# Queries and keys of an attention kernel: copied from tile to tile per term in place of a trip through DRAM, with their projections moved close to their use

## What is computed

```python
qkv = x @ w_qkv                                  # x: 4, 512, 256
q, k, v = (qkv[:, :, 0], qkv[:, :, 1], qkv[:, :, 2])
scores = jnp.einsum('bqhd,bkhd->bhqk', q / scale, k)
scores = jnp.where(causal_mask[None, None], scores, NEG)
attn = jax.nn.softmax(scores, axis=-1)
out = jnp.einsum('bhqk,bkhd->bqhd', attn, v) @ w_out
```

## Time and profile before

| | us |
|---|---|
| time, median of 3 runs | 477.55 |
| lowest and highest | 477.39, 483.26 |
| span of the profiled execution, first to last instruction | 420.8 |
| PE busy in it | 377.7 (90%) |
| DVE busy | 287.1 (68%) |
| POOL busy | 235.4 (56%) |
| DMA, mean rate over the span | 178 GB/s |

### The profile page before, as it was taken

One profiled execution on the slowest core, in us unless ns is written; L12 is line 12 of the kernel. 1 busy time (PEld: TensorE's weight loads), 2 busy tenths in 40 slices (PEclk: granted clock), 3 DMA queues, 4 the chain that ended last, 5 costly groups with the idle time before them and its releaser, 6 DMA issues.

```text
span 420.8 us, 10405 instructions
## 1 busy us (share of the span) xinstructions
PE 377.7 (90%) x2894; PEld 223.1 (53%) x2894; DVE 287.1 (68%) x1009; ACT 242.4 (58%) x534; POOL 235.4 (56%) x374
## 2 busy tenths in 40 slices
PE   5979999999999999997989899988999999989780
PEld 2526554444565445653444466665676777665230
DVE  1157767887879789889799489763666666643562
ACT  2431566667555776556857447562666666556842
POOL 5422144444223888227872855777777766646762
PEclk9999999999999999999999999996999999999987
DMA  4858555646751282649547435636655554429693
GB/s 137 261 192 231 172 165 173 189 136 209 213 164 29 90 277 91 190 144 276 176 149 224 138 123 149 189 132 195 188 175 169 165 158 145 129 69 369 235 375 118
DMA packets 54071, 74.78 MB, mean 178 GB/s; under 512 B 9842, under 2 KB 45308, under 8 KB 52480
## 3 DMA queue, kind: packets, MB, share of 16 engines
q1 hardware_dynamic: 46832, 56.93, 45.7%
q0 software_dynamic: 6912, 16.93, 11.0%
q10 hardware_dynamic: 272, 0.26, 0.2%
HBM read 46.33 MB, written 29.66 MB: 181 GB/s over the span
## 4 chain that ended last, share of the span: by engine, by line
PE 64%; DVE 16%; issue 7%; DMA 6%; ACT 3%; SPq 1%; POOL 1%; ACTq 0%; DVEq 0%
PE PS L697 12%; PE PS L868 8%; PE PS L719 7%; PE PS L821 6%; PE PS L790 5%; PE PS L847 5%; PE PS L665 5%; PE PS L804 3%; DVE MX L1425 2%; PE PS L928 2%; PE PS L710 2%; PE PS L898 2%; DMA YL<-scratch_y 2%; DMA scratch_qk<-PA 1%; DMA scratch_y<-Y,XG 1%
## 5 line engine op out<-in xcount | busy, mean ns | idle before, releaser
L1139 ACT ACTIVATE PT<-PS 128x512 f32<-128x512 f32 x160 | 92.0, 596 | 41.7 <-PE PS L847 36.9
L1783 POOL DMA_INDIRECT scratch_y<-Y,XG x80 | 79.5, 994 | 35.6 <-issue 18.2
L1755 POOL TENSOR_SCALAR_AFFINE_SELECT PT<-PT 128x256 f32<-128x256 f32 (+1 forms) x140 | 50.1, 367 | 78.0 <-ACT PT L1139 76.3
L1774 POOL DMA_INDIRECT scratch_slots<-XP,RI x64 | 63.8, 997 | 35.1 <-DVE XP L1368 16.1
L821 PE MATMUL PS<-KS,QS 96*128 96x512 bf16 (+3 forms) x256 | 61.7, 302 | 10.9 <-DVE MX L1432 4.6
L697 PE MATMUL PS<-W,XGT 128*64 x320 | 61.8, 337 | 1.2 <-DVE WG L1289 0.7
L847 PE MATMUL PS<-QS,KS 98*128 98x512 bf16 (+3 forms) x256 | 60.9, 299 | 1.5 <-ACT PT L1139 1.5
L699 PE MATMUL PS<-WG,XGT 128*64 128x192 f32 x320 | 61.9, 338 | 0.0
L1353 DVE SCALAR_TENSOR_TENSOR HH<-PS,XG,SG 128x96 f32<-128x96 f32 x80 | 24.9, 316 | 35.7 <-ACT SG L1061 31.0
L697 PEld LDWEIGHTS PS<-W,XGT 128*64 128x64 f32 x320 | 41.2, 139 | 13.7 <-issue 9.0
L821 PEld LDWEIGHTS PS<-KS,QS 96*128 96x128 bf16 x256 | 21.4, 99 | 44.7 <-DVE MX L1432 16.7
(11 more groups left out here) (237 smaller groups left out, 718.3 us busy)
## 6 DMA issues: line engine op xcount, KB each, us to landing
XG<-scratch_slots SPq DMA_DIRECT2D x160, 65.0 KB
scratch_qk<-PA SPq DMA_DIRECT2D x14, 384.0 KB, 3.4
W<-in_gate_up_dram SPq DMA_DIRECT2D x16, 288.0 KB
KS<-scratch_qk SPq DMA_DIRECT2D x32, 128.0 KB, 3.5
YL<-scratch_y SPq DMA_DIRECT2D x8, 512.0 KB, 7.0
QS<-scratch_qk SPq DMA_DIRECT2D x8, 384.0 KB, 3.7
QS<-scratch_qk SPq DMA_DIRECT2D x24, 128.0 KB, 3.6
W<-in_down_dram SPq DMA_DIRECT2D x8, 288.0 KB
```

The costliest lines, as they stand in the source:

```text
L1139: e.activation(PT[:, p % NPT, n, :], PS[:, 2 + (rank[u] - 1) % 2, :], ACT.Exp).then_inc(st_exp, 1)
L1755: e.affine_select(out=d, in_=d, compare_op=ALU.is_ge, fill=0.0, base=0, pattern=[[0, 1 if n < 2 else 2], [1, 128]], channel_multiplier=-1) ...
L1774: e.indirect_dma_start(out=XS[:, :], out_offset=bass.IndirectOffsetOnAxis(ap=RI[:, b % 2, TOPK * q + n:TOPK * q + n + 1], axis=0), in_=XP[ ...
L1783: e.indirect_dma_start(out=YK[:, :], out_offset=bass.IndirectOffsetOnAxis(ap=XG[:, j % NXG, D + 1:D + 2].bitcast(I32), axis=0), in_=Y[:, j ...
```

## The change

The scratch tensor in DRAM is gone. A unit `lay` takes the place of `qkout` and `load`: for each of its projection's terms, as soon as that term is there, it copies PA straight into each row of QS or KS where the term is wanted, one DMA of 128 KB per row, six per unit. The lists QS_TERMS and KS_TERMS say which rows take which term. A `lay` first waits until the group three before has done its last `st`, since it writes that group's place of QS and KS. ACT may write a place of PA when the six copies of the unit two before have landed.

The projections of group g stand at the slots 20g - 18 (queries) and 20g - 12 (keys), for all groups from 2 on. Nothing of sequence 1 is projected ahead of slot 0. The values of sequence 1 stand whole at the slots 5 and 9, `xg` of sequence 0 whole at 13. The ones and the input of sequence 1 are issued on SP only behind the four `lay` of sequence 0. The halves of units are gone.

```diff
-QS_ROWS = ((0, 2, 3, 0), (1, 6, 1, 1), (3, 6, 1, 1), (5, 6, 1, 2))
-KS_ROWS = ((0, 3, 2, 1), (1, 6, 1, 0), (2, 6, 1, 0), (5, 6, 1, 0), (4, 6, 1, 2))
+TERMS = 6
+QS_TERMS = ((0, 2, 4), (1, 3), (5,))
+KS_TERMS = ((1, 2, 5), (0, 3), (4,))
+COPIES = 16 * TERMS
...
-    plan = [("inputs",), ("xt", 1)]
+    plan = [("inputs",)]
...
-            put(slot + 3, ("qkout",) + u[1:])
+            put(slot + 3, ("lay",) + u[1:])
...
-                plan += [(kind, 0, m) for kind in ("qk", "resid", "part", "qkout")]
-            plan += [("load", 0), ("v", 0, 0), ("v", 0, 1)]
+                plan += [(kind, 0, m) for kind in ("qk", "resid", "part", "lay")]
+            plan += [("v", 0, 0), ("v", 0, 1)]
...
+            plan += [("ones",), ("xt", 1)]
...
+            for c in range(2):
+                put(5 + 4 * c if b == 1 else VALUES_AT[b - 2] + 2 * c, ("v", b, c))
             if b == 1:
...
+                put(13, ("xg", 0))
+            for half in range(2):
+                put(20 * (2 * b + half) - 18, ("qk", b, half))
+                put(20 * (2 * b + half) - 12, ("qk", b, 2 + half))
...
-    for g in range(2, 2 * B):
-        put(5 * (4 * g - 3), ("load", g))
...
+        def laid(b, m):
+
+            return (ks_in if m >= 2 else qs_in)[m % 2], COPIES * (b + 1)
...
+                elif kind == "lay":
                     b, m = a
-                    r = (rank[u] - 1) % 2
...
+                    g = 2 * b + m % 2
+                    r, rows = (rank[u] - 1) % 2, (KS if m >= 2 else QS)[g % RG]
                     wait_st_group(e, g - RG)
...
+                    for n, part in enumerate((part0, part1, part2)):
+                        e.wait_ge(part, rank["qk", b, m])
+                        for t in (KS_TERMS if m >= 2 else QS_TERMS)[n]:
+                            e.dma_start(rows[t:TERMS * HD:TERMS, :, :], PA[:, r, n, :]).then_inc(laid(b, m)[0], 16)
...
-                    e.wait_ge(ld_in[r], 144 * (g // RG + 1))
+                    e.wait_ge(*laid(g // 2, g % 2))
+                    e.wait_ge(*laid(g // 2, 2 + g % 2))
...
+            order = [u[1:] for u in plan if u[0] == "qk"]
...
-                        e.wait_ge(sc_out[r], stored(w - 2))
+                        e.wait_ge(*laid(*order[w - 2]))
```

More of the change, by code:

```diff
@@ L116, in run_slot @@
         for entry in due:
-            if entry[1][0] in MISC or entry[1][0] == "half":
+            if entry[1][0] in MISC:
                 if not most:
@@ L361, in build @@
         n_misc = 0
-        waiting = None
         for u in plan:
-            assert waiting in (None, u) or u[0] not in MISC, "another unit between a unit's halves"
-            waiting = u[1:] if u[0] == "half" else None if u == waiting else waiting
             kinds[u[0]] = kinds.get(u[0], 0) + 1
@@ L381, in build @@
         part0, part1, part2 = sem("part0"), sem("part1"), sem("part2")
-        sc_out = [sem(f"sc_out{r}") for r in range(2)]
-        ld_in = [sem(f"ld_in{r}") for r in range(RG)]
+        qs_in = [sem(f"qs_in{r}") for r in range(2)]
+        ks_in = [sem(f"ks_in{r}") for r in range(2)]
         max_full, max_free = sem("max_full"), sem("max_free")
@@ L525, in _ @@
                     e.dma_start(WQ[:, :, 2 * D:3 * D], w_v).then_inc(wv_in, 16)
+                elif kind == "ones":
                     wait_const(e, "ones")
@@ L533, in _ @@
                     if b >= 2:
+                        e.wait_ge(*full(("qk", b - 2, 3)))
                         e.wait_ge(*full(("v", b - 2, 1)))
@@ L578, in _ @@
                             e.wait_ge(*full(("v", B - 1, v)))
-                            e.wait_ge(sc_out[v], stored(kinds["qk"] - 2 + v))
+                        e.wait_ge(*full(("qk", B - 1, 3)))
                         e.wait_ge(*full(("xg", B - 1)))
+                        for m in range(4):
+                            e.wait_ge(*laid(B - 1, m))
                     if lo >= 15:
@@ L766, in _ @@
                     keep_busy(idle[u])
-                whole = u[1:] if kind == "half" else u
-                what, a = whole[0], whole[1:]
-                parts = (0,) if kind == "half" else ((1,) if ("half",) + u in rank else (0, 1))
-                if what in MISC:
-                    k = 6 + bank[whole][0]
-                    done = misc_full[bank[whole][0]]
+                if kind in MISC:
+                    k = 6 + bank[u][0]
+                    done = misc_full[bank[u][0]]
                 if u == ("open", 0):
@@ L782, in _ @@
                     gate_and_up(0)
-                elif what == "qk":
+                elif kind == "qk":
                     b, m = a
-                    if 0 in parts:
-                        wait_misc(e, whole)
+                    wait_misc(e, u)
                     e.wait_ge(wq_in[m], 16)
-                    for c in parts:
+                    for c in range(2):
                         e.wait_ge(xt_in[b][c], 16)
@@ L791, in _ @@
                                      start=(c == 0), stop=(c == 1))
-                    if kind != "half":
-                        t.then_inc(done, 1)
-                elif what == "v":
+                    t.then_inc(done, 1)
+                elif kind == "v":
                     b, half = a
-                    if 0 in parts:
-                        wait_misc(e, whole)
+                    wait_misc(e, u)
                     e.wait_ge(wv_in, 16)
@@ L800, in _ @@
                         e.wait_ge(xt_in[b][c], 16)
-                    for q in parts:
+                    for q in range(2):
                         t0 = 128 * (2 * half + q)
@@ L888, in _ @@
                     t.then_inc(done, 1)
-                elif what == "xg":
+                elif kind == "xg":
                     b, = a
-                    if 0 in parts:
-                        wait_misc(e, whole)
+                    wait_misc(e, u)
                     e.wait_ge(gt_in, 16)
@@ L895, in _ @@
                         e.wait_ge(xt_in[b][c], 16)
-                    for q in [2 * n + q for n in parts for q in range(2)]:
+                    for q in range(4):
                         for c in range(2):
```

48 lines of the change are left out of this document (2 added, 46 removed).

## The result

| | before | after |
|---|---|---|
| time, median of 4 runs, us | 478.70 | 499.81 |
| lowest and highest, us | 477.39, 483.26 | 496.66, 504.80 |
| span of the profiled execution, us | 420.8 | 494.9 |
| end of slot 19 | 45.64 | 48.45 |
| end of slot 159 | 217.32 | 239.97 |

The change makes the kernel slower: ratio 1.0377, 95% interval [1.0293, 1.0461]. I had forecast 1.7% slower (485.8 us, 478 to 491). The time lies outside that range: the direction is right, the size more than twice the forecast. The ratios of this text leave out executions over 1.5% above the fastest of their kernel (the longest of them is one of 580.53 us, of `a_late_w`), so they are not the quotients of the medians, here 1.0441.

A forecast was written before the change was run, and what follows sets the result against it. PE, busy 90% of the span, was taken as the bound, the DRAM trip bounding only the start. Start 3.2 plus middle 5.0 made 8.2 us, carried to the 477.55 us median: 485.8 us, 1.7% slower, range 478 to 491.

The forecast's parts named there:

- The start: Slots 0 to 19: first maximum some 3 us earlier, then a wait for late input; end at 48.9, 3.2 us later.
- the half pace: Values of sequence 1, after PE's stall: PE at its lower clock, 3.4 us in place of 1.7.
- The rival in which the gain of the start stays: Start: input of sequence 1 not late, slots 0 to 19 end at 39.3, 6.3 us earlier; 476.2 us; chance 0.05.
- the price of the late input: Start: input of sequence 1 queued behind 24 copies and the ones lands at 31.5; PE stands from about 24.5.
- The copies cost nothing in the middle: Behind the start: nobody waits for the copies' bytes, keys are projected 12 slots ahead; cost nothing.
- Late copies, the rival: First score of a group: PE waits if POOL or SP is over 1.1 us late; 492 us; chance 0.12.
- Slots 20 to 59 no different: Slots 20 to 59: four projections before and four after, so no difference in time.
- Four projections cost 5.0 us: Behind slot 59, eight projections instead of four: three at 1.42 us, slot 82 at 0.7; ends 2.8 and 6.9.
- Spread projections free: Middle: projections in gaps of slots 40 to 60 and the four later ones cost nothing; 477.9 us; chance 0.11.
- The time of before: Whole kernel: the 8.2 us difference on the 420.8 us span was carried unchanged to the median of 477.55.
- The reason given for it ahead of the prediction: Whole kernel: some 57 us of the time lie before the first and after the last instruction.

The follow-up runs named there:

- a_late_w: Changed kernel with input and ones early and the second to fifth late weight DMAs spread to slots 140, 145, 150, 155; 491.58 us, ratio 1.0131.
- a_busy2: Changed kernel with 42 dummy matmuls on PE ahead of the values of sequence 1; 445.81 us, ratio 1.0547 to the kernel before.
- a_early: Changed kernel with the input of sequence 1 and the ones issued ahead of the copies, as before; 435.19 us, ratio 1.0325.
- b_slots: Kernel before, DRAM trip kept, with projections of groups 4 to 7 at 20g - 18 and 20g - 12 and loads seven slots ahead; 450.35 us, ratio 1.0652.
- b_twice: Kernel before with PE doing the four matmuls of each projection of sequence 3 twice; 429.09 us, ratio 1.0161.
- a_free2: Repeat of a_free: changed kernel, input and ones early, projections of groups 5 and 7 four slots earlier; 483.04 us, ratio 0.9969.
- a_xg: Changed kernel with the gate logits of sequences 2 and 3 five slots later (95 and 136); 442.59 us, ratio 1.0476.
- a_free: Changed kernel with input and ones early and projections of groups 5 and 7 four slots earlier, first run; 480.16 us, ratio 0.9997.
- hybrid: Copies for groups 0 to 3 with input and ones early, DRAM and projections of the kernel before for groups 4 to 7; 481.44 us, ratio 0.9952.
- halves: As hybrid, with each of the eight projections in slots 22 to 57 cut into halves in two successive slots; 421.24 us, ratio 0.9985.

## Why the prediction was right and wrong

**The start: right.** First maximum 19.87 (forecast 19.3 to 20.3), 0.64 us per copy (0.62), landing 2.4 (1.8 to 3.6), values at 31.86 (31.5) in 3.75 us (3.4), slot 19 at 48.45 (48.9). Part of the closeness is luck: from the end of the values to slot 19 it took 12.8 us, where I had 14.0, and the values ended 0.7 us later than forecast. (At 0.70 us per copy my own sum puts the input at 33.4, not 33.8.) That the half pace is due because PE stood still is shown by a_busy2. The rival in which the gain of the start stays had 39.3 for slot 19; a_early gave 39.53, so the price of the late input was sized right too.

**The copies cost nothing in the middle: right.** Neither PE nor ACT waited for one behind the start; SP did once, 1.5 us, ahead of the weights. Late copies, the rival, did not come; b_slots shows that the trip through DRAM would have been late at the same distance, by 2.0 to 4.7 us.

**Slots 20 to 59 no different: near.** 42.34 against 42.54 us; 44.02 where the lower clock of slots 25 to 29 comes in.

**Four projections cost 5.0 us: wrong, and this is the step that failed.** The slots 60 to 159 took 147.50 us instead of 129.14, 18.4 more. Of them 6.9 are PE's price (b_twice), 1.9 more than my term: I took 1.42 from a difference of pairs, in one of which I had DVE, not PE, as the full engine, and for slot 82 the remainder alone, 0.7, where PE's 1.72 were due. But 6.9 was the high end of my term, so this alone leaves the time inside the range. What takes it out is a term that the sum doesn't have. 9.7 us more go away when the projections of groups 5 and 7 stand four slots earlier and push nothing aside (147.50 - 137.77 in a_free2, where input and ones are early too; from a_early, which has them early as well, it is 10.5 to 12.0). 5.6 to 8.1 of them are the slots 90 to 94: a bank wait of 2.79 us and the half pace behind it. I had looked at what the moved unit costs, not at what its slot held: the limit of one shared bank unit per slot was in front of me, and that it moves `proj`, and with `proj` the row `fix`, `find`, `mark` in front of the remainder, I didn't follow. a_xg shows that the wait is for the bank; no run leaves the projection at slot 88 and moves `mark` alone back. That leaves 1.7 us (3.2 by a_free), whose place no run shows.

**Spread projections free: refuted.** b_twice, hybrid and halves give 1.7 to 1.9 us each.

**The time of before.** I carried the difference from the span of one chip to the times of another. The difference in us is similar in both (slot 159: 22.7 to 24.9 in the three profiles of the changed kernel; times, by the ratio 18 us and by the medians 21.1 where before takes 479, 23.9 for a_busy2 where it takes 422), so this step did little harm to the forecast. The reason given for it ahead of the prediction was false, so that was luck.

**In sum:** forecast +8.2 at slot 159; measured +22.65 = 2.8 (start) + 1.5 (slots 20 to 59, the lower clock of some executions) + 6.9 (PE) + 9.7 (pushed aside) + 1.7 (open), 22.6 by rounding.

## What to carry to other kernels

On an engine that is busy nine tenths of the time, price a moved piece at its full busy time (here 1.72 us, not 1.42 or 0.7), and check the price by doing it twice where it stands. Then write down what every slot around the new place held before, since a rule such as one shared buffer per slot passes the shift on to units that have nothing to do with the change. A wait behind the wrong neighbour can cost twice: here 2.79 us of stall, and 6.8 us at the lower clock after it.
